# Attention products of a fused attention and FFN kernel: two quads over 256 tokens, rest product in 64-row tiles

## The reference

```python
x = x + layernorm(attn(layernorm(x), ln_w, ln_b, w_q, w_kv, w_o, theta))
x = x + layernorm(ffn(layernorm(x), weight, bias))
```

```python
qk = einsum('bhkd,bhqd->bhkq', q, k) * HD ** -0.5
t = 1.0 + qk + 0.5 * qk * qk
attn = t / sum(t, axis=-1)
wv = einsum('bhkq,bhqd->bhkd', attn, v)      # then @ w_o
```

## Time and profile before

| | |
|---|---|
| median of 3 runs | 645.59 us (644.71 to 646.18) |
| the profiled execution | 645.33 us, of it 643.7 from the first to the last instruction |
| TensorE (PE) busy | 615.6 us, 6660 products |
| VectorE (DVE) busy | 594.8 us |
| ScalarE (ACT) busy | 530.3 us |
| GpSimd (POOL) busy | 449.9 us |
| granted TensorE clock, mean | 0.994 |
| transfers | 43.53 MB, 68 GB/s |

### The profile page before, as it was taken

One profiled execution on the slowest core, in us unless ns is written; L12 is line 12 of the kernel. 1 busy time (PEld: TensorE's weight loads), 2 busy tenths in 40 slices (PEclk: granted clock), 3 DMA queues, 4 the chain that ended last, 5 costly groups with the idle time before them and its releaser, 6 DMA issues. The chain is left out here.

```text
span 643.7 us, 20804 instructions
## 1 busy us (share of the span) xinstructions
PE 615.6 (96%) x6660; PEld 459.2 (71%) x6660; DVE 594.8 (92%) x1489; ACT 530.3 (82%) x1448; POOL 449.9 (70%) x785
## 2 busy tenths in 40 slices
PE   8889999899999999999999999999999999999974
PEld 6766667676686777777777777767777766778763
DVE  6999989899899999999999999999999999987796
ACT  4358788788798897989888888978888888999984
POOL 3565476567777778787877777766877777765454
PEclk9999999999999999999999999999999999999997
DMA  7101022222223332332313222223223211230101
GB/s 247 34 3 42 20 78 57 44 68 61 53 74 85 80 81 75 76 87 62 74 53 85 85 72 80 68 58 111 51 71 90 76 39 42 75 85 19 67 27 50
DMA packets 52362, 43.53 MB, mean 68 GB/s; under 512 B 7200, under 2 KB 48544, under 8 KB 52256
## 3 DMA queue, kind: packets, MB, share of 16 engines
q1 hardware_dynamic: 51440, 41.42, 23.9%
q10 hardware_dynamic: 816, 0.79, 0.4%
HBM read 18.65 MB, written 8.39 MB: 42 GB/s over the span
## 5 line engine op out<-in xcount | busy, mean ns | idle before, releaser
L1168 ACT ACTIVATE feat<-ps_f 128x512 f32<-128x512 f32 x256 | 144.5, 599 | 4.9 <-PE ps_f L852 4.3
L691 DVE TENSOR_TENSOR kf<-kf 128x896 f32<-128x896 f32 (+1 forms) x128 | 132.0, 1033 | 1.8
L852 PE MATMUL ps_f<-qT,selr 128*128 128x512 f32 x320 | 122.1, 435 | 1.6 <-ACT qT L1236 1.3
L691 POOL TENSOR_TENSOR kf<-kf 128x224 f32<-128x224 f32 x64 | 76.5, 1195 | 13.3 <-DVE kf L1515 13.0
L1015 PEld LDWEIGHTS ps_mt<-kf,vp 128*32 128x32 f32 x2048 | 63.7, 109 | 29.7 <-issue 28.2
L1015 PE MATMUL ps_mt<-kf,vp 128*32 128x153 f32 x2048 | 79.0, 294 | 0.8 <-DVE kf L691 0.8
L1725 POOL TENSOR_TENSOR qsp<-kf,qsp 128x256 fp32r<-128x256 f32 x64 | 57.8, 903 | 9.8 <-ACT qsp L1259 9.6
L852 PEld LDWEIGHTS ps_f<-qT,selr 128*128 128x128 f32 x320 | 52.8, 190 | 14.9 <-issue 11.0
L913 PE MATMUL ps_o<-feat,main 120*32 120x512 f32 x448 | 59.7, 604 | 0.0
L916 PE MATMUL ps_o<-feat,rm 128*32 128x512 f32 x448 | 58.6, 593 | 0.0
L1737 POOL TENSOR_TENSOR kf<-kf 128x128 f32<-128x128 f32 x64 | 38.2, 596 | 25.6 <-DVE kf L1508 25.5
(11 more groups left out here) (199 smaller groups left out, 1887.4 us busy)
## 6 DMA issues: line engine op xcount, KB each, us to landing
xc<-L_attn_x SPq DMA_DIRECT2D x16, 512.0 KB, 4.5
result<-fin SPq DMA_DIRECT2D x64, 128.0 KB, 2.0
xa<-L_attn_x SPq DMA_DIRECT2D x15, 512.0 KB, 4.3
heads_out<-osb SPq DMA_DIRECT2D x224, 32.0 KB, 2.0
shares<-sums SPq DMA_DIRECT2D x112, 64.0 KB
sums<-osb SPq DMA_DIRECT2D x224, 2.0 KB
wkqv<-L_attn_w_kv ACTq DMA_DIRECT2D x2, 256.0 KB, 4.5
xa<-L_attn_x SPq DMA_DIRECT2D x1, 384.0 KB, 5.8
```

Of the source, the lines that this page charges most:

```text
L691: return eng.tensor_tensor(dims(row, F_MAIN, [[FW, heads], [HD, NR - 1], [1, HD]]), dims(row, F_LIN, [[FW, heads], [0, NR - 1], [1, HD]]), ...
L852: pe.matmul(ps_f[i % 2][:, :], selr[:, i], queries, start=True, stop=True).then_inc(sel_done, 1)
L1168: act.activation(feat[:, p2, i], ps_f[i % 2][:, :], ACT.Square).then_inc(squared, 1)
```

## The change

A unit of attention is now two quads, p and p + 2, over 256 tokens (half a sequence). The four units of a sequence are (half, p) with half = unit // 2, p = unit % 2. The tail keeps its tiles of 128 tokens.

- `fold_kq` writes the folded q weights in another order of heads, so that a group of 64 columns holds two heads of quad p and two of quad p + 2. A selection reads two groups over 256 tokens and has 512 columns as before.
- `attend` writes two banks: quad p to the first half of ps_o, quad p + 2 to the first half of ps_f[1]. Main is eight products of 256 columns. The rest matrix is stored as 64 rows for each quad, and rest is eight products with 64 rows: rows 0 to 63 to ps_o, rows 64 to 127 to ps_f[1].
- New waits: a selection into ps_f[1] waits for the copy of attend's part there (`f_copied`), attend waits for the squares of the selections 1 and 3 already issued, `copy_quad` for two signals of attend.
- `copy_quad` is two activations of 256 columns; `move_quad` moves two quads for half of the tokens with as many transfers.
- `rest_matrix` and `copy_rest` write the new layout with the same number of instructions (L1033, L1037, L1197).
- On VectorE `constant` is cut into `sum_linear` and `constant`, `rest_terms` into `scale_terms` and `rest_terms`.
- `weight_size` waits for the turned weights; `drain` uses the other bank.
- All tables of `ORDER` are new. In the old steady state PE's list for a tile is: turn_ffn_input, attend, sum_features, select_2, project_v, ffn, select_3, turn_q, select_4, project_kq, turn_z, select_0, select_1, project_out. In the new one: select_2, sum_features, attend, turn_ffn_input, project_kq, select_3, select_4, project_v, ffn, select_0, select_1, turn_q, project_out, turn_z. The idle products of the start (`IDLE["fill"]`) go from 10 places to 15, two products each.

The diff without the tables and small moves:

```diff
@@ fold_kq
-                        mm = pe.matmul(fold_bank(o)[:, :], turn[:, o, c], wkqv[:, c, 0:2 * D], start=c == 0, stop=c == CH - 1)
+                        pe.matmul(fold_bank(o)[:, 0:D], turn[:, o, c], wkqv[:, c, 0:D], start=c == 0, stop=c == CH - 1)
+                    for side in range(2):
+                        for c in range(CH):
+                            mm = pe.matmul(dims(fold_bank(o)[:, :], D + side * HQ * HD, [[P, CH], [1, HQ * HD]]), turn[:, o, c],
+                                           dims(wkqv[:, c], D + side * VW, [[HQ * HD, CH], [P, 2], [1, VW]]), start=c == 0, stop=c == CH - 1)
@@ select
-                    pe.wait_ge(qT_copied, t.n if t.n > BODY else NT * (t.seq + 1))
+                    pe.wait_ge(qT_copied, t.n if t.n > BODY else NT * t.seq + 2 * (quad // 2 + 1))
                 wait(pe, squared, CHUNKS * n + i - 1 if i else CHUNKS * n)
-                queries = qT[:, par, :, quad * P:(quad + 1) * P] if t.n > BODY else qT[:, par, quad]
+                if i % 2:
+                    attend_bank_is_free()
+                half, p = quad // 2, quad % 2
+                queries = (qT[:, par, :, quad * P:(quad + 1) * P] if t.n > BODY
+                           else qT[:, par, 2 * p:2 * p + 2, half * 2 * P:(half + 1) * 2 * P])
@@ attend
+            def feature_bank_is_free():
+
+                if issued["select_1"]:
+                    pe.wait_ge(squared, CHUNKS * (issued["select_1"] - 1) + 2)
+                if issued["select_3"]:
+                    pe.wait_ge(squared, CHUNKS * (issued["select_3"] - 1) + 4)
+
             def attend(t):
...
                 wait(pe, o_copied, issued["attend"])
                 pe.wait_ge(rm_copied, t.seq + 1)
-                pe.wait_ge(squared, CHUNKS * (n + 1))
...
-                for h in range(HQ):
-                    pe.matmul(ps_o[VW * h:VW * (h + 1), :], main[0:NP, par, quad, VW * h:VW * (h + 1)], feat[0:NP, p2, h],
-                              start=True, stop=False, skip_group_check=True)
-                for h in range(HQ):
-                    mm = pe.matmul(ps_o[VW * h:VW * (h + 1), :], rm[:, par, quad, VW * h:VW * (h + 1)], feat[:, p2, HQ],
-                                   start=False, stop=True, skip_group_check=True)
+                pe.wait_ge(squared, CHUNKS * t.n)
+                feature_bank_is_free()
+                pairs = range(CH) if t.n > BODY else [t.tile % 2]
+                for p in pairs:
+                    for e in range(2):
+                        for j in range(HQ):
+                            pe.matmul(attend_bank(e)[VW * j:VW * (j + 1), part(p)], main[0:NP, par, p + 2 * e, VW * j:VW * (j + 1)],
+                                      feat[0:NP, p2, 2 * e + j % 2, tokens(p, j)], start=p == pairs[0], stop=False, skip_group_check=True)
+                for p in pairs:
+                    for j in range(HQ):
+                        for e in range(2):
+                            rows = slice(e * P // 2, (e + 1) * P // 2)
+                            mm = pe.matmul(attend_bank(e)[VW * j:VW * (j + 1), part(p)], rm[rows, par, p, j],
+                                           feat[rows, p2, HQ, tokens(p, j)], start=False, stop=True, skip_group_check=True)
+                            if p == pairs[-1] and j == HQ - 1 and e == 0:
+                                mm.then_inc(first_done, 1)
                 mm.then_inc(quad_done, 1)
@@ copy_quad
-                act.activation(osb[:, par, quad], ps_o[:, :], ACT.Identity, bias=cb[:, par, quad:quad + 1]).then_inc(o_copied, 1)
+                part = slice(half * 2 * P, (half + 1) * 2 * P)
+                act.activation(osb[:, par, p + 2, part], attend_bank(1)[:, 0:2 * P], ACT.Identity,
+                               bias=cb[:, par, p + 2:p + 3]).then_inc(f_copied, 1)
+                act.activation(osb[:, par, p, part], attend_bank(0)[:, 0:2 * P], ACT.Identity,
+                               bias=cb[:, par, p:p + 1]).then_inc(o_copied, 1)
@@ move_quad
-                for part in range(NT):
-                    sp.dma_start(sums[part * H + HQ * quad:part * H + HQ * (quad + 1)],
-                                 osb[HD:P:VW, par, quad, part * P:(part + 1) * P]).then_inc(sums_in, 16)
+                half, p = quad // 2, quad % 2
+                for part in (2 * half, 2 * half + 1):
+                    for qd in (p, p + 2):
+                        sp.dma_start(sums[part * H + HQ * qd:part * H + HQ * (qd + 1)],
+                                     osb[HD:P:VW, par, qd, part * P:(part + 1) * P]).then_inc(sums_in, 16)
```

More of the change, by code:

```diff
@@ L50 @@
     "tensor": (58, {
[L51 to L64, removed]
@@ L835, in drain, with attend_bank_is_free @@
                 pe.wait_ge(squared, CHUNKS * TILES)
-                idle_products(ps_f[1], 2)
+                idle_products(ps_f[0], 2)
+            def attend_bank_is_free():
+                wait(pe, f_copied, issued["attend"])
             def select(t, i):
@@ L888, in turn_z, with part, tokens @@
                 mm.then_inc(zT_done, 1)
-            def attend(t):
-                par, p2, quad = t.par, t.two, t.tile
-                n = t.n - 1
+            def feature_bank_is_free():
[3 more added lines that the diff above has]
+                    pe.wait_ge(squared, CHUNKS * (issued["select_3"] - 1) + 4)
+            def attend(t):
+                par, p2 = t.par, t.two
+                def part(p):
+                    return slice(p * P, (p + 1) * P) if t.n > BODY else slice(0, 2 * P)
+                def tokens(p, j):
+                    g = 2 * p + j // 2
+                    return slice(g * P, (g + 1) * P) if t.n > BODY else slice(j // 2 * 2 * P, (j // 2 + 1) * 2 * P)
@@ L1030, in rest_matrix @@
                 pe.wait_ge(rest_ready, t.seq + 1)
[L1032 to L1033 removed]
+                for g in range(HQ):
+                    pe.matmul(ps_mt[0][VW * g:VW * (g + 1), 0:P], cmat,
+                              dims(main[0:NP, par], g // 2 * 2 * P + g % 2 * VW, [[P, CH], [2 * VW, 2], [1, VW]]),
                               start=True, stop=False, skip_group_check=True)
[L1035 to L1038 removed]
+                for p in range(CH):
+                    for side in range(2):
+                        for g in range(HQ):
+                            j = 2 * side + g % 2
+                            mm = pe.matmul(ps_mt[0][VW * g:VW * (g + 1), VW * (2 * p + side):VW * (2 * p + side + 1)],
+                                           rest[:, p + 2 * (g // 2)], ident[:, VW * j:VW * (j + 1)],
+                                           start=False, stop=True, skip_group_check=True)
                 mm.then_inc(ps_done, 1)
@@ L1194, in copy_rest @@
                 act.wait_ge(ps_done, t.seq + 1)
-                for h in range(HQ):
-                    rows = slice(VW * h, VW * (h + 1))
-                    ins = act.activation(rm[rows, mpar, :, rows], ps_mt[0][rows, 0:P].rearrange("p (a b) -> p a b", a=NQ), ACT.Copy)
+                for g in range(HQ):
+                    rows = slice(VW * g, VW * (g + 1))
+                    ins = act.activation(rm[rows, mpar, :, g % 2:HQ:2], ps_mt[0][rows, 0:P].rearrange("p (a c b) -> p a c b", a=CH, c=2),
+                                         ACT.Copy)
                 ins.then_inc(rm_copied, 1)
@@ L1530, in constant, with scale_terms @@
                                          ALU.mult, ALU.add).then_inc(cb_ready, 1)
-            def rest_terms(t):
+            def scale_terms(t):
                 dve.wait_ge(mt_copied, t.seq + 1)
@@ L1638, in step @@
             def step(n):
+                once(n, "sum_linear", sum_linear)
                 once(n, "constant", constant)
@@ L1662, in step @@
                 setup(n, "weight_scales", weight_scales)
+                once(n, "scale_terms", scale_terms)
                 once(n, "rest_terms", rest_terms)
```

503 lines of the change are left out of this document (252 added, 251 removed), and 101 rows, old and new, of the table ORDER.

## The result

The changed kernel takes **638.35 us** (median of 4 runs, 635.88 to 640.14) beside 645.46 us of the kernel before on the same chip: ratio 0.9887, 95% interval [0.9852, 0.9923]. On another chip it was 637.39 beside 645.52, ratio 0.9893 [0.986, 0.9926]. It is 7.1 us faster, where 16.6 were forecast: the direction and the range were right, the size was not.

What follows compares the result with a forecast made beforehand. PE's amount of work was taken as the bound, with DVE close behind: 645.3 us, less 20.2 of PE stream (27.5 - 6.7 - 0.6), plus 4 given back, makes 629 us; own range 622 to 636, whole range 618 to 644.

Steps and rivals of the forecast that it cites:

- the sum of 20.2 us for PE's stream: PE's whole stream: 27.5 us gained on rest, less 6.7 for shape changes and 0.6 for main.
- the rest costs nothing on the path: ACT's half copies, DVE's split steps, transfers, setup fold and start idle products: all covered by idle time or waits, 0 us.
- The row halves side by side: Rest product in attend: both 64-row halves run at once, two rounds, 0.43 us a unit instead of 0.86.
- rival 3: Rest product: row halves don't run side by side, rest stays at 0.86 us, kernel takes 652.6 us; chance 0.07.
- Rest: Rest product in attend: falls from 0.86 to 0.43 us a unit, 27.5 us gained over 64 units.
- Main: Main product in attend: four rounds instead of two over the same columns, 0.01 us a unit, 0.6 us lost.
- Changes of shape: PE's tile shape changes: 198 before, 265 after, 67 more at 0.10 us each, 6.7 us lost.
- DVE takes 4 us back: Middle of the kernel: DVE close behind PE; PE's idle time taken as twice 4.2 us, 4 us given back.
- The idle products at the start: Kernel start: ten more would cost 3 us if PE weren't waiting for inputs there, which it is for 3.2 us.
- the end itself is only moved, not changed: Last tile: the chain of waits ends in add_ffn, long after the last attend, so the end keeps its form.
- The shared bank: PE's new waits at attend and select_3: about 1 us left for ACT each, stall 0; deciding from 0.32 us a unit.
- an edit is worth what it takes from PE's stream: Whole kernel: PE's amount of work sets the end, so its savings count, as long as DVE can follow.

Runs made afterwards that it cites:

- e2: Changed kernel with the rest matrix on all 128 rows, zeros in the other half, so rest takes four rounds: 648.11 us, ratio 1.0038 to the kernel before.
- e3: Changed kernel run with the order tables and start idle products of the kernel before: 718.72 us, ratio 1.1127.
- e15: Kernel before with half of the rest product's columns worked twice in the 56 body units: 665.35 us, ratio 1.0306.
- e1: Kernel before with half of the rest product left out in all 64 units: 640.61 us, ratio 0.993.
- e5: Kernel before with VectorE's second group of pair products over three heads instead of six from the third tile on: 642.89 us, ratio 0.9966.
- e6: Kernel before with both half of the rest product left out and VectorE's second pair products over three heads instead of six: 630.14 us, ratio 0.9776.
- e13: Changed kernel unchanged, run again with a second trace: 637.39 us, ratio 0.9893; the traced execution took 638.30 us.
- e16: Changed kernel without the twelve idle products ahead of the weight fold at the start: 637.93 us, ratio 0.9896 to the kernel before.

## Why the prediction was wrong in size

Two steps failed: the sum of 20.2 us for PE's stream, which measures 13, and "the rest costs nothing on the path", which measures 3 us at the two ends.

- **The row halves side by side** (rival 3): right, eight tiles within 0.04 us.
- **Rest**: its two rounds take 0.48 us where 0.43 was put, so this term is 0.38 us a unit, 24.3 in place of 27.5. **Main**: the two more rounds cost nothing to be seen (0.86 to 0.87 us in e2, 0.88 before).
- **Changes of shape**: the count was right, 67 more (199 and 266 in the traces). The two new ones, before and behind rest, take 0.12 and 0.11 us, against 0.10 taken. The one that falls away behind sum_features gives 0.05 (1.15 to 1.10 us by the medians) and not 0.10. With rest this makes 0.20 us a unit (0.26 in the one shown) in place of 0.315: the sum of 20.2 us should have been 13, 17 at most. The Trainium skill, "TensorEngine Tiling (Array Packing)", section Tiling Modes, has a change drain TensorE; the runs agree, also for a change of rows alone (0.98 against 0.86 us for main, e2).
- **DVE takes 4 us back**: in size about right for the body, where 10 to 11.5 us stay, and PE's idle time in the middle went from 4.2 to 7.7 us, much as was put. But what it rested on failed: DVE's idle time there did not fall to 5 to 8 us, it rose to 21.2. That the size came out is luck in so far as the price of PE's work depends on the order (below).
- **"The rest costs nothing on the path"**: failed at the ends, by 1.5 to 2.2 us at the start and 1.4 to 3.9 behind the last sum_features. The idle products at the start were costed at nothing because PE was waiting for inputs; PE waited elsewhere, not ahead of the fold. The clock at the end was not costed at all: "the end itself is only moved, not changed".
- **The shared bank**: its stall of 0 was right with the new tables (1.6 and 1.4 us in all), and its price was judged too low for the case where it decides (e3: 62 us).
- **The rule beneath it all does not hold as it was put**: "an edit is worth what it takes from PE's stream". 415.76 us busy of 420 says that added work costs most of itself (0.83, e15), not that removed work comes back: in the old order 0.18 of it did, and PE and DVE held each other (e1, e5, e6); in the new order 0.61 of the row tiles' 16 us did (e2). Busy PE is also no measure of its stream: that is 13 us shorter, PE's busy time by 5.0, since a start that comes late by less than the instruction ahead lasts leaves no idle time in the profile. That the changed kernel gets 10 to 11.5 us in the body, where e1, with more taken from PE, gets 6.1, thus goes with its new tables; what these do to the old program, without the two banks, was not tried.

The account for 7.1 in place of 16.6, by e13's trace, the execution of 638.30 us: some 7 us of stream that were never saved and 2.9 us at the two ends, less 1 us, since the body gave back 2.9 (10.1 of 13 us stay) and not 4.

## What to carry to other kernels

When one engine is 99% busy in a hand-written order, read the second engine before pricing an edit: if it is as close behind as here (403 us busy of 420, beside 416), work taken from the first alone may give a fifth of itself, while work added costs most of itself. Price the first and the last stretch by themselves, with the granted clock, since a change of order moves them even when the body alone is meant. Operands and order are one design: the same program cost 80 us more in the old order. The end differs by 2.5 us between two traces of the changed kernel alone: look at when the clock fell in each.

## What the hardware showed unexpectedly

- Eight tiles of 64 rows by 32 columns, in two banks, take 0.24 us a round of 256 fp32 columns; four tiles of 128 by 32 take 0.22.
- A change from 120 rows to 64, with the columns at 32, costs 0.12 us, about as much as one back to full width (0.11).
- When the granted clock falls differs between executions of one kernel: at 618.9 us in the changed kernel's first trace, at 627.6 in its second, where PE's idle gaps of 1.56 us (at 621.96) and 1.39 us (at 625.23) lie ahead of the fall. With 18 idle products in these gaps it fell behind PE's last product in four traces of four, and without them in e16.
- With VectorE's product over half as many heads, GpSimd's own product, unchanged, took 1002 ns in place of 1195 (e5).
